# First attention: one gathered column in 99 fetched row by row by SyncE, and its stores issued by ScalarE

## What is computed

```python
h = (x @ W).reshape(N, H, F)              # N = 6250, H = 4, F = 64
e = leaky_relu(h_l[row] + h_r[col], 0.2)  # one edge each, 100000 edges
ex = exp(e - segment_max(e, row)[row])
att = ex / segment_sum(ex, row)[row]
out = segment_sum(att[:, :, None] * h[col], row)
```

## Time and profile before

| | us |
|---|---|
| median of 3 runs | 2603.76 |
| lowest, highest | 2602.64, 2607.0 |
| profiled execution | 2602.79 |
| its span | 2600.8 |

### The profile page before, as it was taken

How to read it: one execution, slowest core, us unless ns; L and a number is a source line. 1 busy time by engine, 2 the same in 40 slices (tenths; PEclk the granted TensorE clock), 3 DMA queues, 4 the chain that set the end, 5 groups by cost and what they waited for, 6 DMA issues and landing times. The chain is left out here.

```text
span 2600.8 us, 26571 instructions
## 1 busy us (share of the span) xinstructions
PE 1829.4 (70%) x7736; PEld 1419.5 (55%) x7740; DVE 1951.5 (75%) x3922; ACT 679.2 (26%) x1487; POOL 1685.7 (65%) x1747
## 2 busy tenths in 40 slices
PE   4621623555545454667567999999999899999638
PEld 3420202434434342334345778888888788888537
DVE  8888977999777888767676757766777666666747
ACT  7710001323222222133232521111211111121136
POOL 0000777777777777777754777777777777777460
PEclk9955866767777676888787889999999999999869
DMA  5121226657656666576667731222222222222567
GB/s 173 58 16 47 65 67 198 225 190 243 221 197 220 197 220 203 177 246 214 207 213 270 185 82 35 61 49 49 49 49 61 39 59 49 49 49 43 179 213 284
DMA packets 153243, 354.36 MB, mean 136 GB/s; under 512 B 55065, under 2 KB 95695, under 8 KB 143459
## 3 DMA queue, kind: packets, MB, share of 16 engines
q1 hardware_dynamic: 68161, 189.12, 20.4%
q0 software_dynamic: 68672, 120.59, 20.0%
q10 hardware_dynamic: 16324, 43.71, 4.4%
HBM read 180.24 MB, written 172.06 MB: 135 GB/s over the span
## 5 line engine op out<-in xcount | busy, mean ns | idle before, releaser
L649 POOL DMA_INDIRECT at_ring<-table,e_col x732 | 697.5, 953 | 223.1 <-issue 223.1
L2223 POOL DMA_INDIRECT at_ring<-table,at_idx x693 | 679.2, 980 | 211.1 <-issue 210.8
L2315 PE MATMUL at_psS<-at_ring,at_hot 128*128 128x260 f32 x1584 | 436.5, 439 | 94.5 <-DVEq L2421 87.2
L2315 PEld LDWEIGHTS at_psS<-at_ring,at_hot 128*128 128x128 f32 x1584 | 318.9, 218 | 203.7 <-issue 82.0
L1638 PE MATMUL ffn_psH<-xnT,ffn_space 128*128 (+1 forms) x896 | 362.6, 548 | 0.3 <-ACT ffn_space L1705 0.3
L919 DVE SCALAR_TENSOR_TENSOR pick_prod<-const_iota,pick_tile,pick_rows 128x400 f32<-128x400 f16 x292 | 171.0, 627 | 252.3 <-PE pick_rows L899 243.0
L2337 ACT ACTIVATE at_ring<-at_psS 128x520 f32<-128x520 f32 (+1 forms) x432 | 237.7, 567 | 465.2 <-PE at_psS L2315 465.0
L1651 PE MATMUL ffn_psY<-ffn_space 128*128 128x256 f32 x1568 | 358.8, 381 | 0.0
L1651 PEld LDWEIGHTS ffn_psY<-ffn_space 128*128 128x128 f32 x1568 | 299.5, 191 | 53.2 <-issue 13.4
L1705 ACT ACTIVATE ffn_space<-ffn_psH,ffn_b 128x448 f32<-128x448 f32 x224 | 129.7, 630 | 667.7 <-PE ffn_psH L1638 667.6
L1638 PEld LDWEIGHTS ffn_psH<-xnT,ffn_space 128*128 128x128 f32 x896 | 268.3, 311 | 47.7 <-issue 2.3
(11 more groups left out here) (438 smaller groups left out, 2557.4 us busy)
## 6 DMA issues: line engine op xcount, KB each, us to landing
at_sums<-at_ring SPq DMA_DIRECT2D x72, 1452.0 KB, 6.0
products<-ffn_space ACTq DMA_DIRECT2D x28, 512.0 KB
at_ring<-table,e_col POOLq DMA_INDIRECT x831
at_sums<-at_ring SPq DMA_DIRECT2D x16, 768.0 KB
late_space<-products SPq DMA_DIRECT2D x24, 512.0 KB, 6.3
at_ring<-table,at_idx POOLq DMA_INDIRECT x693
products<-ffn_space ACTq DMA_DIRECT2D x28, 384.0 KB
late_space<-products SPq DMA_DIRECT2D x24, 384.0 KB, 6.6
```

The costliest lines, as they stand in the source:

```text
L649: g.indirect_dma_start(self.ring[z][:, k, 0:TW], None, self.table, bass.IndirectOffsetOnAxis(ap=self.runs.col[:, u * U + k:u * U + k + 1], ...
L2223: g.indirect_dma_start(self.ring[z][:, k, 0:self.TW], None, self.table, bass.IndirectOffsetOnAxis(ap=self.idx[:, z, k:k + 1], axis=0)).the ...
L2315: last = pe.matmul(self.psS[at % 2][:, k - lo, 0:TW], self.hot[:, b, k, :], rows[:, b * self.SUB + k, 0:TW], start=True, stop=True)
```

## The change

Column 32 of group 0 is no longer gathered by GpSimd in rounds 1 to 7 (round 0 is as before). SyncE brings it: it waits until block 2 of group 0 of the round before is stored, then loads row numbers from a DRAM list `lanes` into 16 registers at a time, and issues one DMA per row, 127 in a round, from `table` to one partition of `ring[0]`. Their semaphore `s_lane` counts 16 for each row. The DRAM list is filled once in `fill`, from an intermediate result of VectorE in `rowf` (the columns' node numbers of the chains), for which VectorE now writes the masked codes to `rowf` and waits (`s_plain`) before it uses `rowf` again. All that SyncE issued in the loop before (tails, stores, own terms, carry) is now issued by ScalarE, in its own order: the tail before weigh, each store right after the six copies of its block, own terms or carry behind the last store. The last round is taken out of ScalarE's loop. Whoever waits for the landed rows of group 0 waits for two semaphores.

```diff
+BY_ROW, AT_ONCE = (0,), 16
@@ ChainRuns.fill
+        sp.wait_ge(self.s_plain, 1)
+        for n, z in enumerate(BY_ROW):
+            row = z * WIDE + WIDE - 1
+            sp.dma_start(self.att.lanes[n:n + 1, :], self.rowf[row:row + 1, :].bitcast(I32)).then_inc(self.s_lanes, 16)
+        sp.wait_ge(self.s_lanes, 16 * len(BY_ROW))
+        sp.sem_inc(self.s_plain, 1)
@@ ChainRuns.vector
-        do(v.tensor_scalar(self.colf.bitcast(I32), code, (1 << COL_BITS) - 1, None, ALU.bitwise_and))
-        do(v.tensor_copy(self.colf, self.colf.bitcast(I32)))
+        do(v.tensor_scalar(self.rowf.bitcast(I32), code, (1 << COL_BITS) - 1, None, ALU.bitwise_and))
+        v.sem_inc(self.s_plain, 1)
+        do(v.tensor_copy(self.colf, self.rowf.bitcast(I32)))
...
+        v.wait_ge(self.s_plain, 2)
@@ ChainAttend.gather
-        for k in range(WIDE):
+        for k in range(WIDE - (z in BY_ROW)):
@@ ChainAttend
+    def rows_landed(self, eng, n, z):
+        less = z in BY_ROW
+        eng.wait_ge(self.s_rows[z], n(16 * (WIDE - less), 16 * WIDE))
+        if less:
+            eng.wait_ge(self.s_lane[z], n(16 * LIVE, 0))
+
+    def row_by_row(self, sp, r, z, registers):
+        sp.wait_ge(self.s_stored[z][self.NSUB - 1], r * 16 + 16)
+        sp.sem_inc(self.s_pad_sync, 1)
+        for lo in range(0, LIVE, AT_ONCE):
+            hi = min(lo + AT_ONCE, LIVE)
+            at = BY_ROW.index(z)
+            sp.reg_load(registers[0:hi - lo], self.lanes[at:at + 1, bass.ds(r * LIVE + lo, hi - lo)])
+            for lane in range(lo, hi):
+                node = sp.snap(registers[lane - lo], min_val=0, max_val=self.table.shape[0] - 1)
+                sp.dma_start(self.ring[z][lane:lane + 1, WIDE - 1, 0:self.TW], self.table[bass.ds(node, 1), :])\
+                    .then_inc(self.s_lane[z], 16)
@@ ChainAttend.sync (the loops of bring_tail, store and finish are gone)
+        registers = [sp.alloc_register(f"lane_{i}") for i in range(AT_ONCE)]
+        with sp.Fori(1, K) as r:
+            for z in BY_ROW:
+                self.row_by_row(sp, r, z, registers)
@@ ChainAttend.bring_scores
-        pe.wait_ge(self.s_rows[z], n(16 * WIDE, 16 * WIDE))
+        self.rows_landed(pe, n, z)
@@ ChainAttend.take_sums
+            self.store(a, n, z, b)
+        if own_units is None:
+            self.keep_carry(a, z)
+        else:
+            self.next_own(a, n, z, own_units)
@@ the stream of ScalarE, rounds 5 to 7
-                    with a.Fori(0, rest) as r:
+                    with a.Fori(0, rest - 1) as r:
                         n = counter(r, SHORT_ROUNDS + TURNING)
                         for z in range(GROUPS):
+                            att.bring_tail(a, n, z)
                             att.weigh(a, n, z)
-                            att.take_sums(a, n, z)
+                            att.take_sums(a, n, z, found.units)
+                    for z in range(GROUPS):
+                        att.bring_tail(a, counter(0, chains.steps - 1), z)
+                        att.weigh(a, counter(0, chains.steps - 1), z)
+                        att.take_sums(a, counter(0, chains.steps - 1), z)
```

More of the change, by code:

```diff
@@ L1967, in __init__ @@
         self.s_new, self.s_runs = sem("new_made"), sem("runs_by_group")
+        self.s_plain, self.s_lanes = sem("plain"), sem("lanes")
     def load(self, sp):
@@ L2178, in __init__ @@
         self.nothing, self.s_nothing, self.s_blank = sb("nothing", [1, W]), sem("nothing"), sem("nothing_made")
+        self.lanes = nc.dram_tensor(f"{tag}_lanes", [len(BY_ROW), x.M], I32, kind="Internal").ap()
+        self.s_lane = {z: sem(f"lane{z}") for z in BY_ROW}
         self.ring = [sb(f"ring{z}", [P, WIDE, W]) for z in range(GROUPS)]
@@ L2226, in sync @@
     def sync(self, sp, own_units):
-        x, K, TW = self.index, self.index.steps, self.TW
-        sums = self.sums[0:x.rows, :].rearrange("(l c) w -> l c w", l=P)
+        x, K = self.index, self.index.steps
         sp.wait_ge(self.s_blank, 2)
         sp.dma_start(self.sums[x.rows:x.rows + 1, :], self.nothing[:, :]).then_inc(self.s_nothing, 16)
-        SUB, NP, blocks = self.SUB, len(self.pairs), self.NSUB
-        per = blocks * NP + 1
         for z in range(GROUPS):
             sp.dma_start(self.own[z][:, :, :].rearrange("p l h -> p (l h)"), own_units[0, z, :, :]).then_inc(self.s_own[z], 16)
[L2236 to L2269, removed]
-        for z in range(GROUPS):
[L2272 to L2277, removed]
@@ L2278, in sync @@
-        finish(K - 1, 0, GROUPS - 1, False)
-        for z in range(GROUPS):
-            for b in range(blocks):
+        registers = [sp.alloc_register(f"lane_{i}") for i in range(AT_ONCE)]
+        with sp.Fori(1, K) as r:
+            for z in BY_ROW:
+                self.row_by_row(sp, r, z, registers)
+        for z in range(GROUPS):
+            for b in range(self.NSUB):
                 sp.wait_ge(self.s_stored[z][b], 16 * (K + 1))
@@ L2284, in sync, with sums_by_lane, bring_tail, store @@
         sp.wait_ge(self.s_nothing, 16)
+    def sums_by_lane(self):
+        return self.sums[0:self.index.rows, :].rearrange("(l c) w -> l c w", l=P)
+    def bring_tail(self, a, n, z):
+        self.rows_landed(a, n, z)
+        for b in range(self.NSUB):
+            a.wait_ge(self.s_stored[z][b], n(16, 16))
+        a.dma_start(self.ring[z][LIVE:P, :, 0:self.TW],
+                    self.sums_by_lane()[LIVE - 1:LIVE, bass.ds(n(CHAINS, z * WIDE - CHAINS), WIDE), 0:self.TW])\
+            .then_inc(self.s_tail[z], 16)
+    def store(self, a, n, z, b):
+        NP = len(self.pairs)
+        per = self.NSUB * NP + 1
+        a.wait_ge(self.s_out, n(GROUPS * per, z * per + 1 + (b + 1) * NP + 2))
+        a.dma_start(self.sums_by_lane()[:, bass.ds(n(CHAINS, z * WIDE + b * self.SUB), self.SUB), :],
+                    self.ring[z][:, b * self.SUB:(b + 1) * self.SUB, :]).then_inc(self.s_stored[z][b], 16)
+    def next_own(self, a, n, z, own_units):
+        a.dma_start(self.own[z][:, :, :].rearrange("p l h -> p (l h)"),
+                    own_units[bass.ds(n(1, 1), 1), z, :, :].rearrange("o i n -> (o i) n")).then_inc(self.s_own[z], 16)
+    def keep_carry(self, a, z):
+        a.dma_start(self.carry[z * WIDE:(z + 1) * WIDE, :], self.ring[z][LIVE - 1:LIVE, :, :]).then_inc(self.s_carry, 16)
     def begin_tensor(self, pe):
@@ L2328, in weigh, with take_sums @@
         a.activation(self.ring[z][:, :, TW:W], self.highest, ACT.Copy).then_inc(self.s_out, 1)
-    def take_sums(self, a, n, z):
+    def take_sums(self, a, n, z, own_units=None):
         rows, TW, NP = self.ring[z], self.TW, len(self.pairs)
@@ L2790, in _ @@
                         att.weigh(a, n0, z)
-                        att.take_sums(a, n0, z)
+                        att.take_sums(a, n0, z, found.units)
                     with a.Fori(0, TURNING) as r:
@@ L2794, in _ @@
                         order2.copy_over(a, r * 2)
+                        att.bring_tail(a, n, 0)
                         att.weigh(a, n, 0)
                         order2.copy_back(a, r * 2)
-                        att.take_sums(a, n, 0)
+                        att.take_sums(a, n, 0, found.units)
                         order2.copy_over(a, r * 2 + 1)
+                        att.bring_tail(a, n, 1)
                         att.weigh(a, n, 1)
-                        att.take_sums(a, n, 1)
+                        att.take_sums(a, n, 1, found.units)
                         order2.copy_back(a, r * 2 + 1)
+                        att.bring_tail(a, n, 2)
                         att.weigh(a, n, 2)
-                        att.take_sums(a, n, 2)
+                        att.take_sums(a, n, 2, found.units)
                     found2.load_prior(a)
-                    with a.Fori(0, rest) as r:
+                    with a.Fori(0, rest - 1) as r:
                         n = counter(r, SHORT_ROUNDS + TURNING)
                         for z in range(GROUPS):
+                            att.bring_tail(a, n, z)
                             att.weigh(a, n, z)
-                            att.take_sums(a, n, z)
+                            att.take_sums(a, n, z, found.units)
[3 more added lines that the diff above has]
+                        att.take_sums(a, counter(0, chains.steps - 1), z)
                 @block.vector
```

2 lines of the change are left out of this document (1 added, 1 removed).

## The result

The changed kernel takes 2995.07 us in the median of 4 runs, 2605.38 before beside it (4 runs); the ratio is 1.1487, 95% interval 1.1469 to 1.1505: 390 us slower. The forecast was slower, but 2731 us, with a range up to 2894. Its profiled execution took 2994.96 us with a span of 2993.3.

What follows compares the result with a forecast made beforehand. GpSimd's gathers, nearly balanced with compute, were taken as the bound; SyncE's 84.4 us of rows would miss group 0's windows, 125.3 us later, plus 3 for ScalarE's issuing: 2602.8 + 128.3 = 2731 us, range 2602 to 2894.

Steps and rivals of the forecast that it cites:

- The bound and the prize: First attention's gather stage: GpSimd and compute nearly balanced; seven gathers of 1.285 us removed, at most 9.0 us won.
- The windows and the processing: Group 0, block-2 store to next round's bring_scores: SyncE has 48 to 86 us; lateness adds up over six cycles, 125.3 us.
- P: Processing of group 0 from bring_scores to its block-2 store, 43.1 to 61.2 us a round, 307.5 in sum.
- The price of a row: SyncE's single-row DMA: 0.31 us issue (index load L1973's figure) plus register work, 0.52 us a row, 66.6 us for 127.
- The register loads: SyncE's row numbers: 8 loads of up to 16 a round, one 2.1 us round trip each, 16.8 us.
- T: SyncE's time for all 127 rows of a round, row numbers included: 84.4 us, forecast range 54 to 108.
- Rival 4: Register loads on SyncE cost a trip per register, 0.42 us each: T 121, 380 us later, 2985 us; 5%.
- The issuing on ScalarE: Stores, own loads and tails moved from SyncE: idle time covers most, nine late stores cost 3 us (0 to 10).
- 1: SyncE keeps up and GpSimd stays the bound: T under 46 us, time 2597 us; 8%.
- 2: SyncE's rows fall between: T of 46 to 54 us, within 5 us of now, some 2605 us; 8%.
- 3: SyncE's row issue costs 0.81 us as in the one-partition tail: T 148, 568 us later, 3174 us; 7%.
- 5: Rows issued in time land late beside busy DMA engines: 5 us more each cycle, 30 us, inside the range, no own chance.

Runs made afterwards that it cites:

- f1: The changed kernel without its row-by-row column: GpSimd gathers all 99 columns again, ScalarE still issues stores, tails, own terms and carry; 2626.27 us, 1.0073 of the kernel before.

## Why the prediction was wrong, step by step

**The bound and the prize.** GpSimd and compute as nearly balanced: right. 9 us as "the most that the change can win": 5.6 measured.

**The windows and the processing.** Right, and the part that carried the forecast. The predicted times from bring_scores to the landed store (P and 6.0 for the landing), 49.1, 50.7, 53.7, 56.0, 67.2 and 66.8, stand against 47.7, 48.5, 52.4, 53.8, 67.8 and 67.1: 343.5 against 337.3 in sum. That the delay adds up over the rounds, and that everything else fits inside, is shown by the table of the rounds, whose account closes to 1 us. The run for group 2 supports it by its processing (275 us against 273), while its total agrees partly by luck.

**The price of a row.** 0.52 us was too high: issue 0.218 instead of 0.31, which is nearer to the one-row store's 0.24 than to the row I chose, and 0.19 for register work and gaps, as estimated (0.21). 127 x 0.41 = 52 instead of 66.6 us, and 5 to 8 us of stalled issues in most rounds (12 in round 4) that I had not put in.

**The register loads: the term that failed.** I took "one round trip of 2.1 us for each instruction", 16.8 us a round. They took 66 to 68 us in six rounds and 27 in round 4: 8 x (1.12 + 6.9) = 64 by the medians. Two things were missed. The code's one load is two, with 1.1 us for the list's address each time. And a load from an address that is no multiple of 16 bytes takes 6.9 us, or 6.9 / 16 = 0.43 us a register. 50 us a round in six rounds, less some 8 us for the cheaper rows, net of stalled issues, gives T of about 126 where I had 84.4; 126.3 to 131.1 were measured.

Rival 4, "a trip for each register, at a fifth of a trip each, 0.42 us", had the size of this load, and gave 2985; it got 5%. That the total came so near is partly luck: it left out the address loads (9 us a round) and the stalls, had the row 15 us a round too dear, and knew nothing of the quick round 4. Its counter-argument, one instruction for 16 neighbouring words, holds only for the aligned start, where a load takes 2.04 us, very nearly the round trip assumed; that this is one round trip is not shown, and the 2.83 us of the load of 15 speaks against it. My sum with 1.12 us more a load would give a T of 93, and the padded kernel has 91 to 94, but only because its stalls (8 to 12 us) make up for most of the row price set too high.

The Trainium skill's figure, 200 ns a register ("Runtime: NRT & Kernel Launch", section "Instruction fetch mechanics"), lies between the two that these runs show, 128 ns aligned and 432 ns not. The Trainium skill's floor of about 600 ns for a load ("DMA: Bandwidth & Descriptors", section "Latency and other measured facts") is far under both loads of 16 (2.04 and 6.9 us) and under the 1.0 us of the shortest load of one address. The range I gave had T = 108 at its upper end, which let this case fall outside though its price had been worked out.

**The issuing on ScalarE.** "3 (0 to 10)" for the stores: 4.3 measured (1 to 6 by the interval), right. But the tail was put down as free, since only weigh stood behind it on ScalarE. I looked at what is queued behind the moved DMA and not at who waits for its data: weigh_rows on VectorE needs it, and ScalarE issues it only after the group before. 16 us by itself. In the changed kernel weigh_rows waits 59 us for tails too, but the processing there is no longer than forecast, so little of it reaches the time.

**The rivals.** 1 (SyncE keeps up, T under 46) is excluded by 127 x 0.41 = 52 us before any load, and 2 (T of 46 to 54) by the run without loads in the loop, with T of 61 to 68. 3 (0.81 of issue for one partition) fell: 0.218. So the single partition is not what costs in the tail's issue; whether its 33 pieces do is not shown. 5 (late landing): 1.4 us from last issue to bring_scores, nothing.

## What to carry to other kernels

A transfer that may start only after one event and must land before another is priced by its duration against that window, in every round; if the event that opens the next window hangs on its arrival, each microsecond over is paid once a round. Before a step is moved to another engine's queue, look at both sides: what queues behind it there, and who waits for its data when it can be issued only in that engine's order. Scalars that a sequencer reads from memory belong to the critical path like any DMA: align the list, load 16 numbers rather than 15, and read ahead of the wait.

## What the runs showed of the hardware

- A load of 16 registers from DRAM by SyncE (without the eighth of each round, which loads 15) takes 2.0 us in the median where the list's offset is a multiple of 16 bytes (round 4 of the changed kernel, at byte 2032 plus multiples of 64, and all rounds of the padded one), and 7.0 us at multiples of 4 or 8 bytes. A load of 15 takes 2.8 us at the former and 6.0 at the latter. Each comes with a load of the list's address, 1.12 us. Why alignment matters is not shown, only that one word of shift brings the long load back.
- A DMA of one row of 1040 bytes from DRAM to one partition with the row number in a register takes SyncE 0.218 us to issue (0.225 in the run without loads in the loop), 0.41 us with its register work. In a round 5 to 24 of 127 issues take over 0.3 us, up to 1.67 us (padded kernel); what stalls them is not shown.
- A tail of 33 pieces to one partition takes 0.80 us to issue in the median (f1). Where weigh_rows had to wait for it, it started 5.6 to 7.4 us after the issue, although the tail moves 33.5 KB only.
